# Three small moves in a two-layer kernel: expert sums scaled on ScalarE, filler matmuls on TensorE, the last group of the last stage split over two engines

## The chip, the cores and the metric

One core of one Trainium2 chip runs the whole kernel as a single program. The time is device microseconds (us) of that core. The engines are named as in the profile: PE is TensorE (PEld its weight loads), DVE is VectorE, ACT is ScalarE, POOL is GpSimd, SP is SyncE (it only issues DMAs here). L1305 is line 1305 of the kernel before.

## The reference, cut to what matters

4096 tokens of width 128 (2 sequences of 2048) go through four blocks, each as `x = x + layernorm(block(layernorm(x)))`:

```python
x = x + _layernorm(_L0_attn_ref(_layernorm(x)))   # state-space scan, 16 states, over 2048 steps
x = x + _layernorm(_L0_ffn_ref(_layernorm(x)))    # 8 experts, each takes its 512 best tokens
x = x + _layernorm(_L1_attn_ref(_layernorm(x)))   # linear attention, 8 heads of 16, Taylor features
x = x + _layernorm(_L1_ffn_ref(_layernorm(x)))    # 8 experts, each token goes to its best 2
```

The layernorm is `(x - mean) / sqrt(var + 1e-5)` over the 128 features. Everything is fp32.

## The kernel before, in words

The tokens lie on the chip in `X`, 8 groups of 512 tokens (4 tiles of 128 each, `J` = 4, `W` = 512). Each engine has its own instruction stream, written out by hand in the order in which that engine is to do it; streams meet only at semaphores (`wait_ge`). Where a step serves several groups at once, `groups` and `each_group` call it with offsets: `at(0)` is the group of this step, `at(1)` and `at(2)` the next ones, `at(-1)` and `at(-2)` those before. An engine does a step's instructions strictly in the order written, so one that waits holds up all behind it.

The layer-1 attention (scan): PE turns and projects the tokens, DVE makes the scan (L1045 to L1060) and signals `a_hc`. PE then makes outputs in 4 chunks `c` of two sequences `b`: `skips(c)` (the `D * x` term, 8 products of 128 columns, L1595) and `outputs(c)` (8 products with 32 rows, L1602) into PSUM. `skips(0)` and `skips(1)` stand ahead of the wait for `a_hc`. DVE takes the statistics of each (chunk, sequence) (`stats`, L989 to L997), POOL the `-0.5` power, DVE adds the normalised output to `X` (L1080) and takes statistics of the sum; ACT writes the normalised rows (L801), PE turns these (`scores`, L1611) and, when ACT has copied them (L808), multiplies by the router's weights (L1616). ACT copies the scores out (L812). The rows of the last (chunk, sequence) are made by DVE (L1092). The last scores go by a DMA (L816) to the search for the experts' thresholds.

The key pass of the layer-2 attention has 8 steps, one a group, over four engines. Before it the experts' sums are loaded into `acc` (two buffers). Per step, with m = at(0), g = at(1), h = at(2):
- DVE (L1293 to L1334): for g the shift (L1311) and `X += acc * rstd`, four `scalar_tensor_tensor` of 128x128 (L1315); products of m's tile 0 (L1305, L1307); statistics of `X` of g; statistics of `acc` of h; the shift of g (`shift`, L1277); products of m's tiles 1 to 3.
- POOL (L697): power for g (`d_xrstd`), power for h (`d_frstd`, the one by which `acc` is scaled), a product for the logits.
- ACT (L865): eviction of m's four tiles from PSUM (L876, L878) and of the queries (L885), then for g `normalise` (four `activation`, L858), then when PE has turned these, the copy `xnT` (L896).
- PE (L1723): the projections of m (L1730, L1754), the accumulations (L1740), the turning of g (L1763).

The choice of experts of layer 2: after the last group's `mix`, DVE clears `scan[:, 0:1]` (L1438) and casts `choice_b` (L1439), then scans the counts (L1441). When the lists are done (`r_lists`), POOL starts the gathers of the last block (L733), behind four waits, `r_lists` the first (L722 to L725).

The last stage (`finish`): for each of 8 groups the two choices' rows are added (DVE L1547 for the first 4, PE L1918 into a PSUM bank for the last 4: `ysum` products with the identity, 512 columns), DVE takes the statistics, POOL makes the factor (`g_rstd`) and the shift (`g_nmr`), ACT scales four tiles in place (L978) and signals `g_out`, DVE adds to `X` (L1556), and SP stores. DVE does the add of group n two steps after its statistics.

## Time and profile before

| | us |
|---|---|
| median of 3 runs | 719.86 (718.79 to 723.21) |
| the profiled execution | 715.17 |
| its span, first to last instruction | 713.3 |
| PE busy | 518.2 (73%) |
| DVE busy | 426.9 (60%) |
| ACT busy | 332.8 (47%) |
| POOL busy | 313.0 (44%) |
| mean granted TensorE clock | 0.847 |

The profiled execution is 1.87 us longer than its span and 4.69 us under the median of the runs. Times inside the span are counted from its start. A row of the timeline merges neighbouring instructions of one line: start, length, engine, line, what is written and read, count, and in brackets how long the engine sat idle before it and what ended that. An fp32 product on PE stands as two MATMUL records. PEclk is the granted TensorE clock, 1.00 for 2.4 GHz and 0.50 for 1.2 GHz.

### The profile page before, as it was taken

How to read it: one execution, taken by the hardware profiler on the slowest of the kernel's cores; microseconds unless marked ns; L12 is line 12 of the kernel's file. 1: busy time of each engine (PE TensorE's matmuls, PEld its weight loads, DVE VectorE, ACT ScalarE, POOL GpSimd, SP SyncE). 2: the span in 40 equal slices, each digit the busy share in tenths (PEclk: the TensorE clock that was granted, in tenths of full speed). 3: DMA queues.
4: the chain of work that ended last, by engine and by line, in shares of the span. 5: the costliest groups of instructions: out<-in, count | busy, mean ns of one | idle time of the engine just before them, and what ended most of it. 6: DMA issues, size and time to landing. Idle time of an engine off the chain costs nothing.

```text
span 713.3 us, 13599 instructions
## 1 busy us (share of the span) xinstructions
PE 518.2 (73%) x3894; PEld 382.3 (54%) x3896; DVE 426.9 (60%) x1784; ACT 332.8 (47%) x690; POOL 313.0 (44%) x329
## 2 busy tenths in 40 slices
PE   1769610378777508877899997149999999999925
PEld 1457100245544303433334444149999999999921
DVE  4789668835322238898426878883545545455447
ACT  3815510044323115454357663165666666666616
POOL 3514300067878723243001112016777667767535
PEclk9966755569978758899999998559999999999976
DMA  7401272012323350100000100021111111111155
GB/s 189 130 0 56 69 291 123 6 38 41 45 43 43 34 173 28 31 15 1 2 0 16 31 27 20 15 24 42 50 48 49 46 47 48 48 44 49 38 202 167
DMA packets 47736, 42.23 MB, mean 59 GB/s; under 512 B 15346, under 2 KB 41835, under 8 KB 47179
## 3 DMA queue, kind: packets, MB, share of 16 engines
q1 hardware_dynamic: 35770, 25.48, 11.4%
q0 software_dynamic: 10816, 15.82, 10.6%
q10 hardware_dynamic: 1104, 0.39, 0.2%
q8 instruction: 21, 0.34, 0.2%
q14 instruction: 25, 0.20, 0.1%
HBM read 26.23 MB, written 15.30 MB: 58 GB/s over the span
## 4 chain that ended last, share of the span: by engine, by line
PE 45%; DVE 27%; issue 11%; POOL 6%; ACT 5%; DMA 4%; ACTq 1%; DVEq 0%; POOLq 0%; SPq 0%
PE bank L1886 18%; PE bank L1907 9%; DVE st L1259 3%; POOL sum_dram L673 3%; PE bank L1695 2%; PE bank L1740 2%; PE bank L1730 2%; DVE mv L1264 2%; POOL arena L661 2%; DVE st L989 2%; ACT arena L913 1%; POOL rstd L687 1%; PE bank L1796 1%; DVE hit L1103 1%; PE bank L1896 1%
## 5 line engine op out<-in xcount | busy, mean ns | idle before, releaser
L1886 PE MATMUL bank<-arena 128*128 128x128 f32 x1136 | 140.1, 277 | 0.4 <-ACT arena L964 0.4
L1886 PEld LDWEIGHTS bank<-arena 128*128 128x128 f32 x1136 | 133.9, 194 | 0.7 <-ACT arena L964 0.7
L687 POOL TENSOR_TENSOR rstd<-ve,mhalf 128x4 f32<-128x4 f32 x40 | 48.7, 1217 | 167.7 <-DVE ve L1267 121.7
L1519 DVE TENSOR_TENSOR arena<-arena,bank 128x512 f32<-128x512 f32 x71 | 48.8, 688 | 81.4 <-PE bank L1886 81.4
L741 POOL DMA_INDIRECT y_dram<-arena,sidx x71 | 69.9, 985 | 44.4 <-DVE arena L1524 41.1
L950 ACT ACTIVATE arena<-wgu 128x1024 f32 x71 | 75.0, 1057 | 26.5 <-PE bank L1886 26.2
L733 POOL DMA_INDIRECT arena<-x3row_dram,gidx x71 | 68.8, 969 | 36.5 <-issue 20.7
L1907 PE MATMUL bank<-w,arena 128*128 x568 | 75.1, 275 | 0.0
L1907 PEld LDWEIGHTS bank<-w,arena 128*128 128x128 f32 x568 | 69.1, 192 | 0.2 <-issue 0.2
L956 ACT ACTIVATE arena<-bank 128x512 f32<-128x512 f32 x71 | 42.4, 597 | 42.7 <-PE bank L1886 42.7
L673 POOL DMA_INDIRECT sum_dram<-arena,idx x32 | 50.7, 1585 | 15.2 <-issue 7.6
L661 POOL DMA_INDIRECT arena<-x1row_dram,idx x32 | 31.3, 977 | 59.0 <-DMA x1row_dram<-wtok 49.0
L1241 DVE TENSOR_TENSOR arena<-arena,bank 128x256 f32<-128x256 f32 x32 | 13.5, 421 | 62.9 <-ACT arena L845 52.5
L913 ACT ACTIVATE arena<-bank 128x512 f32<-128x512 f32 x64 | 33.0, 603 | 22.4 <-PE bank L1796 22.4
L1305 DVE TENSOR_TENSOR arena<-arena 128x1024 f32<-128x1024 f32 x32 | 39.1, 1223 | 7.2 <-ACT arena L876 6.9
L1695 PE MATMUL bank<-w,arena 128*128 128x512 f32 x64 | 39.4, 702 | 0.0
L1740 PE MATMUL bank<-arena 128*17 128x153 f32 x512 | 25.5, 324 | 14.2 <-DVE arena L1307 14.1
L1524 DVE TENSOR_SCALAR arena<-bank,wrow 128x128 f32<-128x128 f32 x71 | 24.9, 351 | 11.4 <-PE bank L1907 7.0
L1740 PEld LDWEIGHTS bank<-arena 128*17 128x17 f32 x512 | 12.7, 103 | 32.4 <-issue 18.0
L1632 PE MATMUL bank<-cntb,blk_b 128*128 128x3 bf16 (+1 forms) x17 | 3.2, 186 | 35.7 <-DVE rank L1103 30.0
L1730 PE MATMUL bank<-wqkv,xnf 128*128 128x328 f32 x64 | 26.3, 519 | 1.0 <-ACT xnf L896 0.7
L1690 PE MATMUL bank<-ident,arena 128*128 128x128 f32 x32 | 11.1, 347 | 21.0 <-DMA arena<-x1row_dram,idx 21.0
(326 smaller groups left out, 1049.0 us busy)
## 6 DMA issues: line engine op xcount, KB each, us to landing
wgu<-in_wgu SPq DMA_DIRECT2D x1, 4096.0 KB, 12.2
wgu<-y_dram SPq DMA_DIRECT2D x8, 512.0 KB, 6.7
X<-in_x SPq DMA_DIRECT2D x8, 256.0 KB, 5.6
sum_dram<-zero POOLq DMA_DIRECT2D x8, 256.0 KB, 4.2
x1row_dram<-row SPq DMA_DIRECT2D x8, 256.0 KB, 2.4
w<-in_w SPq DMA_DIRECT2D x1, 2048.0 KB, 17.4
acc<-sum_dram SPq DMA_DIRECT2D x8, 256.0 KB, 2.9
w<-in_wd SPq DMA_DIRECT2D x1, 2048.0 KB, 10.2
```

What stands on the lines that cost most here:

```text
L661: nc.gpsimd.indirect_dma_start(xg[:, n % XG], None, x1row_dram, bass.IndirectOffsetOnAxis(ap=idx[:, e, k:k + 1].bitcast(U32), axis=0)).the ...
L673: nc.gpsimd.indirect_dma_start(sum_dram, bass.IndirectOffsetOnAxis(ap=idx[:, e, k:k + 1].bitcast(U32), axis=0), yw[:, n % 8], None, comput ...
L687: nc.gpsimd.tensor_tensor(out, ve[:, u], mhalf[:, 0:J], ALU.pow).then_inc(done, 1)
L733: nc.gpsimd.indirect_dma_start(xr[:, n.ring], None, x3row_dram, bass.IndirectOffsetOnAxis(ap=gidx1[:, n.n:n.n + 1].bitcast(U32), axis=0)). ...
L741: nc.gpsimd.indirect_dma_start(y_dram, bass.IndirectOffsetOnAxis(ap=sidx1[:, o.n:o.n + 1].bitcast(U32), axis=0), yr[:, o.ring], None).then ...
L950: nc.scalar.activation(wnow[:, k.pair], wgu[:, ds(e, 1)].rearrange("p o n -> p (o n)"), ACT.Copy).then_inc(f_w, 1)
L956: nc.scalar.activation(sgl[:, m.pair], bank[1 + m.pair][:], ACT.Silu).then_inc(f_silu, 1)
L1519: nc.vector.tensor_tensor(gl[:, m.pair], sgl[:, m.pair], bank[3 + m.pair][:], ALU.mult).then_inc(f_gated, 1)
L1695: nc.tensor.matmul(bank[2 + m.pair][:], xgT[:, m.pair], w13[:, ds(m.lap, 1)].rearrange("p o n -> p (o n)"), start=True, stop=True).then_in ...
L1740: last = nc.tensor.matmul(bank[3 + a.b][32 * q:32 * q + DH + 1, g_ * NF:(g_ + 1) * NF], vx[:, j, h, 0:DH + 1], kx[:, j, h, 0:NF], start=Fa ...
L1886: last = nc.tensor.matmul(bank[first + m.pair][:, h * P:(h + 1) * P], wnow[:, m.pair, at_:at_ + P], xrT[:, m.ring], start=True, stop=True)
L1907: last = nc.tensor.matmul(bank[5 + o.pair][:, 0:D], gl[:, o.pair, h * P:(h + 1) * P], wd[:, ds(e, 1), h].rearrange("p o n -> p (o n)"), st ...
```

## The change

- Key pass: ACT scales `acc` of h by `rstd` in place (four `activation` Copy with a per-partition scale), placed between `normalise` of g and the `xnT` copy of g, and signals `d_scaledsum`; DVE waits for it and does one `tensor_tensor` add of 128x512 in place of the four of L1315.
- TensorE: `keep_warm(n)` issues n products of the identity with `xnTA[:, 0, 0]` (128x512, fp32) into bank 6, which nobody reads. Nine stand behind `skips(1)` and ahead of the wait for `a_hc`, five ahead of `scores(3)`.
- Last stage, last group: DVE scales tiles 2 and 3 from the bank straight onto `X`, signals `g_scaled`, and adds their shift; ACT waits for `g_scaled` and scales tiles 0 and 1 only; DVE then adds 256 columns in place of 512.
- The clearing of `scan` and the cast of `choice_b` move into the last step of the query pass, ahead of DVE's wait for `q_yrstd`.
- POOL's wait for `r_lists` becomes the last of the waits ahead of the first gather.
- `g_scaled` and `d_scaledsum` are semaphores used earlier (`g_sum`, `a_abs`), counted on.

```diff
+        g_scaled, SCALED_BY_DVE = g_sum, GR - BY_DVE
+        d_scaledsum, SCALED = a_abs, CH
...
-            pool.wait_ge(r_lists, LEAD + 2)
             for u in range(2):
                 pool.wait_ge(q_rowst[u], LEAD + 16 * CH)
             pool.wait_ge(f_wst, LEAD + 16)
+            pool.wait_ge(r_lists, LEAD + 2)
...
             def key_pass(at):
-                g, m = at(1), at(0)
+                h, g, m = at(2), at(1), at(0)
...
                     normalise(lambda j: xn[:, g.b, j], tokens(g), g.b).then_inc(d_xn, 1)
+                if h:
+                    act.wait_ge(d_frstd, LEAD + h.n + 1)
+                    for j in range(J):
+                        last = nc.scalar.activation(acc[:, h.b, j], acc[:, h.b, j], ACT.Copy, scale=rstd[:, h.b, j:j + 1])
+                    last.then_inc(d_scaledsum, 1)
+                if g:
                     act.wait_ge(d_xtps, LEAD + g.n + 1)
                     if not early(g, 2):
                         act.wait_ge(d_qkv, LEAD + J * (g.n - 1))
                     nc.scalar.activation(xnT[:, g.b], bank[0][:], ACT.Copy).then_inc(d_xt, 1)
-            groups(act, key_pass, 1, 0, 2)
+            groups(act, key_pass, 2, 0, 2)
...
                 act.wait_ge(g_nmr, LEAD + g.n + 1)
-                for j in range(J):
+                if g.n == GR - 1:
+                    act.wait_ge(g_scaled, LEAD + SCALED_BY_DVE + 1)
+                for j in range(J if g.n < GR - 1 else 2):
...
-                    for j in range(J):
-                        xc = xl[:, ds(g.place, 1), j].rearrange("p o d -> p (o d)")
-                        last = nc.vector.scalar_tensor_tensor(xc, acc[:, g.b, j], rstd[:, g.b, j:j + 1], xc, ALU.mult, ALU.add)
-                    last.then_inc(d_x2, 1)
+                    dve.wait_ge(d_scaledsum, LEAD + SCALED + g.n + 1)
+                    xc = X[:].rearrange("p b c w -> p (b c) w")[:, ds(g.place, 1)].rearrange("p o w -> p (o w)")
+                    nc.vector.tensor_tensor(xc, xc, acc[:, g.b].rearrange("p j d -> p (j d)"), ALU.add).then_inc(d_x2, 1)
...
                 if m:
+                    if m.n == GR - 1:
+                        nc.vector.memset(scan[:, 0:1], 0.0)
+                        nc.vector.tensor_copy(choice_b[:], choice128[:])
                     dve.wait_ge(q_yrstd, LEAD + m.n + 1)
...
-            nc.vector.memset(scan[:, 0:1], 0.0)
-            nc.vector.tensor_copy(choice_b[:], choice128[:])
             dve.wait_ge(r_counts, LEAD + 1)
...
+                if l and l.n == GR - 1:
+                    dve.wait_ge(g_rstd, LEAD + l.n + 1)
+                    for j in range(2, J):
+                        last = nc.vector.scalar_tensor_tensor(xl[:, l.place, j], bank[l.n][:, j * P:(j + 1) * P],
+                                                              rstd[:, l.b, j:j + 1], xl[:, l.place, j], ALU.mult, ALU.add)
+                    last.then_inc(g_scaled, 1)
+                    dve.wait_ge(g_scaled, LEAD + SCALED_BY_DVE + 1)
+                    dve.wait_ge(g_nmr, LEAD + l.n + 1)
+                    for j in range(2, J):
+                        nc.vector.tensor_scalar(xl[:, l.place, j], xl[:, l.place, j], nmr[:, l.b, j:j + 1], None, ALU.add)
                 if l:
                     dve.wait_ge(g_out, LEAD + l.n + 1)
-                    x = xl[:, l.place].rearrange("p j d -> p (j d)")
-                    nc.vector.tensor_tensor(x, x, (ysum[:, l.n, 0] if l.n < BY_DVE else bank[l.n])[:, 0:W], ALU.add).then_inc(g_x, 1)
+                    w = W if l.n < GR - 1 else 2 * P
+                    x = xl[:, l.place].rearrange("p j d -> p (j d)")[:, 0:w]
+                    nc.vector.tensor_tensor(x, x, (ysum[:, l.n, 0] if l.n < BY_DVE else bank[l.n])[:, 0:w], ALU.add).then_inc(g_x, 1)
...
+            def keep_warm(n):
+                for _ in range(n):
+                    nc.tensor.matmul(bank[6][:], ident[:], xnTA[:, 0, 0], start=True, stop=True)
             skips(0)
             skips(1)
+            keep_warm(9)
             pe.wait_ge(a_hc, LEAD + 1)
...
                     outputs(c + 2)
+                if c == CH - 1:
+                    pe.wait_ge(a_x1t, LEAD + 2 * c)
+                    keep_warm(5)
                 scores(c)
```

## Rows read from the trace of the kernel before

**Rows 1.** The page, its part 4: shares of the chain by engine

```profile
PE 45%; DVE 27%; issue 11%; POOL 6%; ACT 5%; DMA 4%; ACTq 1%; DVEq 0%; POOLq 0%; SPq 0%
```

**Rows 2.** Stretches: length; busy PE, PEld, DVE, ACT, POOL; PEclk, DMA share, GB/s

```profile
50.10:76.40 26.30, 22.06 (x101) 16.23 (x100) 24.98 (x178) 12.44 (x28) 13.00 (x13) 0.69 0.16 44
...
258.00:344.00 86.00, 62.70 (x620) 31.60 (x624) 73.56 (x285) 38.61 (x112) 30.59 (x40) 0.85 0.12 38
```

**Rows 3.** Timeline of PE around the wait for the scan

```profile
37.78 3.59 PE L1595 MATMUL bank<-diagD,arena 128*128 128x128 f32 x16 [2.46 <-DVE arena L1032]
46.28 6.50 PE L1602 MATMUL bank<-wout,arena 32*128 32x128 f32 x32 [4.91 <-DVE arena L1060]
...
67.75 2.05 PE L1602 MATMUL bank<-wout,arena 32*128 32x128 f32 x16
```

**Rows 4.** Stretches of PE alone: length; busy (records); PEclk, DMA share, GB/s

```profile
41.00:44.40 3.40, 0.37 (x3) 0.99 0.00 0
44.60:64.90 20.30, 18.07 (x75) 0.50 0.09 26
```

**Rows 5.** The chain in order of time: two 512-column products at full clock

```profile
30.10 1.73 PE bank L1581 x4
```

**Rows 6.** Timeline of DVE: statistics of the first two outputs

```profile
48.40 0.29 DVE L989 BATCH_NORM_STATS2 st<-bank 128x6 f32<-128x128 f32 x1 [2.17 <-issue]
...
50.10 0.29 DVE L989 BATCH_NORM_STATS2 st<-bank 128x6 f32<-128x128 f32 x1 [0.20 <-issue]
```

**Rows 7.** All waits of DVE from 50.1 to 76.4: total, times, longest

```profile
DVE st L989 <- issue: 0.2, 1, 0.2
```

**Rows 8.** Timeline of PE at the end of the stage (scores of chunks 2 and 3)

```profile
79.39 3.18 PE L1616 MATMUL bank<-x1T,wg 128*8 128x512 f32 x4
84.78 0.66 PE L1611 MATMUL bank<-ident,row 128*128 128x128 f32 x4 [2.21 <-ACT row L801]
...
87.08 2.75 PE L1616 MATMUL bank<-x1T,wg 128*8 128x512 f32 x4
```

**Rows 9.** Timeline of ACT in the key pass: one step, and a later half-clock step

```profile
283.37 1.65 ACT L858 ACTIVATE xnf<-X,nmr,rstd 128x128 f32<-128x128 f32 x4 [0.18 <-DVE nmr L1277]
286.00 0.60 ACT L896 ACTIVATE xnf<-bank 128x512 f32<-128x512 f32 x1 [0.98 <-PE bank L1763]
287.77 0.33 ACT L876 ACTIVATE arena<-bank 128x192 f32<-128x192 f32 x1 [1.17 <-PE bank L1730]
...
296.72 0.60 ACT L896 ACTIVATE xnf<-bank 128x512 f32<-128x512 f32 x1 [2.01 <-PE bank L1763]
```

**Rows 10.** Timeline of POOL: the power of the next group's sums, same step

```profile
283.42 1.92 POOL L687 TENSOR_TENSOR rstd<-ve,mhalf 128x4 f32<-128x4 f32 x1 [0.22 <-DVE ve L1267]
```

**Rows 11.** Timeline of DVE: the first group's add, and one step's

```profile
259.16 1.13 DVE L1315 SCALAR_TENSOR_TENSOR X<-acc,rstd,X 128x128 f32<-128x128 f32 x4
...
287.21 1.13 DVE L1315 SCALAR_TENSOR_TENSOR X<-acc,rstd,X 128x128 f32 x4
288.26 1.21 DVE L1305 TENSOR_TENSOR arena<-arena 128x1024 f32<-128x1024 f32 x1
```

**Rows 12.** Groups of ACT by shape: busy us, mean ns, idle before

```profile
L830 ACT ACTIVATE arena<-arena,pcol 128x512 bf16<-128x512 bf16 x8 | 5.8, 722 | 42.2 <-DVE arena L1197 42.2
...
L789 ACT ACTIVATE arena<-arena 128x512 f32<-128x512 f32 x1 | 0.6, 631 | 0.0
```

**Rows 13.** Timeline of the last group of the last stage

```profile
708.35 1.48 ACT L978 ACTIVATE bank<-bank,nmr,rstd 128x128 f32<-128x128 f32 x4 [0.54 <-POOL nmr L754]
709.86 0.69 DVE L1556 TENSOR_TENSOR X<-X,bank 128x512 f32<-128x512 f32 x1 [1.33 <-ACT bank L978]
```

**Rows 14.** Timeline: cast ahead of the scan of counts, and the first gather

```profile
455.59 0.19 DVE L1439 CAST arena<-choice 128x64 bf16<-128x64 f32 x1
...
455.69 0.68 DVE L1441 TENSOR_TENSOR_SCAN arena<-onesW,bank 128x256 f32<-128x256 f32 x1
...
478.02 1.07 POOL L733 DMA_INDIRECT arena<-x3row_dram,gidx  x1 [13.71 <-DVE gidx L1501]
```

## The prediction

> **What bounds the kernel now.** I read the page first, then the chain in order of time, then the timeline engine by engine at the places touched. The page's chain says that no single engine sets the time: PE 45%, DVE 27%, POOL 6%, ACT 5% [rows 1]. So each edit has to be read in its own stage. The long expert stage, where PE is the bound, is not touched. The edits lie in four others:
> - The scan stage of layer 1. From 50.1 to 76.4 DVE is busy 24.98 of 26.30 us, PE 22.06 [rows 2], and DVE's waits there add up to 0.2 us, all of it one wait [rows 7]. DVE sets the pace; PE only matters at the start and at the end.
> - The key pass of layer 2. DVE is busy 73.56 of 86.00 us and ACT only 38.61 [rows 2]. That looks like work to be moved from DVE to ACT. But the loop through a step is DVE's shift, ACT's normalise, PE's turning, ACT's copy, PE's projection, ACT's eviction, DVE's products, so ACT's place in it counts, not its share.
> - The choice of experts and the last stage: short chains.
>
> **Nine fillers ahead of the outputs.** PE ends `skips(1)` at 37.78 + 3.59 = 41.37 and sits idle 4.91 us until the scan is done at 46.28 [rows 3]. A filler is an fp32 product with 512 columns. At full clock two of these took 1.73 us [rows 5], so 0.865 each; nine take 7.8 us. The clock is granted at 0.99 from 41.0 to 44.4 and at 0.50 from 44.6, after PE has stood idle [rows 4]; with fillers in that gap I take it as staying full. The fillers then end at 41.37 + 7.8 = 49.15, 2.9 us after the scan. The first sequence's outputs are 8 records; at full clock 16 took 2.05 us [rows 3], so 1.03. DVE starts at 49.15 + 1.03 + 0.05 = 50.2, against 48.40. The second statistics started at 50.10 after 0.20 of idle time [rows 6], which goes: so +1.8 - 0.2 = +1.6 us on DVE, which has no slack behind it until 76.4 to win it back. Faster products afterwards win nothing, since DVE doesn't wait for them [rows 7]. Bounds: if `skips(1)` ran at full clock (2.05 for 16 records) PE would be free 1.5 us earlier and the loss is 0.1; if the clock falls at 44.5 all the same, it is 7.5 (below). I take 1.6.
>
> **Five fillers ahead of the last scores.** PE ends the scores of chunk 2 at 79.39 + 3.18 = 82.57 and gets the next rows at 84.78 [rows 8]. Five fillers at full clock take 4.3 us and end at 86.9, 2.1 us after the rows. The two turnings follow at 0.6 each, the second copy of ACT at 0.6 runs beside the first product, and two score products at full clock take 1.73: 86.9 + 0.6 + 0.6 (copy of the first) + 1.73 = 89.8. Before, the last product pair was 2.75 us, partly at half clock, and ended at 87.08 + 2.75 = 89.83 [rows 8]. So 0.0. Bounds: -0.7 if the pair before would have been wholly at half clock (2 x 1.73 = 3.46), and +2 if the fillers begin at half clock. I take 0, because the warm products pay back just what the fillers take.
>
> **The key pass.** The price of a scale on ACT is not in the trace with this form. A Copy with one per-partition operand took 722 ns for 512 columns, one with immediates 631 [rows 12], so an operand costs 91 ns. Four 128-column instructions with two operands take 1.65 us [rows 9]: 0.39 from start to start. One operand less gives 0.30, and four give 1.3 us; bounds 0.8 (no price for the operand) and 1.65. On DVE four instructions took 1.13 us and the next starts 1.05 after the first [rows 11]; one add of 512 columns is 0.69 [rows 13], some 0.61 from start to start. DVE wins 0.44 us a step.
>
> Now where ACT does it: after `normalise` of g, before the copy `xnT` of g. In the step shown ACT is done with normalise at 285.0; POOL's power for h ends at 283.42 + 1.92 = 285.34 [rows 10], so ACT waits for it, behind it the copy waits, and behind that PE's projections. The scales run 285.4 to 286.6, the copy starts at 286.6 instead of 286.00 [rows 9]: +0.6. The eviction that DVE needs ended at 287.77 + 0.33 = 288.10, DVE started its products at 288.26 [rows 9, 11]: 0.16 of slack, so +0.44 on the products of tile 0. From these to the next shift nothing shrinks, so the loop grows by 0.44. What DVE saved (0.44) it now waits away ahead of these products. Seven steps have a scale. Four run at full clock (this one; the other three, worked the same way, +0.31 to +0.40): together 1.5. In the others the turning itself is late because PE is at half clock: there the copy starts 3.5 us after normalise began or later (296.72, after 2.01 us of idle time) [rows 9], which covers the scales: 0. A rule of the Trainium skill speaks here against the change: "ScalarE: Activation LUTs", rules for kernel authors, puts multiply and add on VectorE, not ScalarE. By that rule the four scales stay where they were and the sum would be 2.4 us lower; the trace agrees insofar as ACT's four cost 1.3 us where DVE saves 0.44.
>
> The first group has no step ahead of it to hide in. There the chain is POOL's power, DVE's add at 259.16 (1.13) [rows 11], statistics. Now it is power, four scales (1.3), add (0.69): +0.9. Key pass: 1.5 + 0.9 = +2.4. Bounds: -2.2 (scales quite hidden, seven steps at -0.44, first group +0.9), and +5.8 (seven steps at +0.7).
>
> **The last stage.** DVE is free at 709.86 - 1.33 = 708.53 [rows 13]. It scales two tiles (0.28 each from rows 11) until 709.15. ACT waits for that instead of starting at 708.35: two tiles, half of 1.48 plus a start, from 709.2 to 710.0 [rows 13]. DVE's two shifts lie beside it. The add of 256 columns is some 0.4: 710.4 to 710.45, against 710.55. So -0.1, bounds -0.3 to +0.3. Cutting ACT's work in half is nearly eaten by ACT's later start.
>
> **The two reorders.** The cast stood 0.10 us ahead of the scan of counts [rows 14]; ahead of `q_yrstd` it lies in DVE's wait for POOL's power: -0.1 (0 if that wait is short). The first gather starts 0.28 us after the list's last instruction, at 478.02 [rows 14]; three passed waits less behind the last signal: -0.05, bounds -0.2 and 0.
>
> **Sum.** 1.6 + 0 + 2.4 - 0.1 - 0.1 - 0.05 = +3.75, say +3.7. The profiled execution took 715.17, so 718.9 for one like it. The median of the runs shown is 4.69 above it; I add the sum to the median: 719.86 + 3.7 = 723.6.
>
> **Rivals.**
> - DVE stays the bound of the key pass and the scales are hidden. For it: DVE's 86% against ACT's 45%. Against: the products of tile 0 follow the eviction by 0.16 only, and the copy is behind the scales in order. Key pass -2.2 instead of +2.4: 719.0.
> - The fillers carry the full clock to the end of the scan stage. For it: this is what they are placed for, and PE at full clock from 76 would cut the two score pairs from 3.18 and 2.75 to 1.73 each, -2.4: 721.2. Against: PE idles between chunks whatever stands at 41. The Trainium skill ("TensorE: Matmul & The Clock Gate", why this matters for your kernels) says that continuous work keeps the clock up; the trace doesn't bear that out for this work: from 44.6 to 64.9 PE was busy 18.07 of 20.30 us at 0.50 [rows 4].
> - The other side, slower: the clock falls at 44.5 in spite of the fillers. Then 3.1 us of fillers (3.6 of them) run at full clock, 5.4 at 1.73 take 9.3: they end at 53.8. The outputs at half clock add 2.1: DVE starts at 55.9 instead of 48.40, +7.5 instead of +1.6: 729.5. It decides above 1% from the point where more than four of the nine run at half clock. Against: the clock rose by 41.0 on the products of `skips(1)`, and wider ones should hold it.
>
> **Chances.** Forecast 0.60, hidden scales 0.15, full clock to the end 0.11, clock falls 0.10, something else 0.04. About 1% (7.2 us) is what a measurement can tell from no change. The gains even of both good rivals together (716.6) stay within it, so faster by over 1% gets 0.03; slower has the third rival and the upper ends of the key pass and the last scores: 0.13; the rest, 0.84, is within 1%. The range goes from 717.5 (first rival, with the good ends of the small terms) to 729.5 (third rival).
>
> **What would show it.** In the scan stage: the nine fillers end near 49, PE's first L1602 products at full clock, and DVE's wait ahead of the first statistics 3.9 us instead of 2.17. In the key pass: ACT's wait for POOL between normalise and scales, the copy some 3.4 us after normalise starts, DVE idle about 0.8 us ahead of the products of each tile 0, and the full-clock steps 0.4 us longer than before. In the last stage: DVE ends within 0.3 us of before, counted from the first statistics. I am wrong if the fillers end before 47, if DVE doesn't wait in the key pass, or if those steps are shorter than before.

## The result, and the profile after

| | before | after |
|---|---|---|
| median | 718.73 us (715.70 to 723.21, 20 runs) | 723.52 us (717.42 to 729.34, 20 runs) |
| ratio of the two | | 1.0059, 95% interval 1.0041 to 1.0076 |
| profiled execution | 715.17 us, span 713.3 | 725.88 us, span 724.0 |
| mean granted clock | 0.847 | 0.852 |

The change costs 0.59% (0.41 to 0.76), some 4.2 us; the medians differ by 4.79. The forecast was +3.7 us and 723.6. One of the 20 executions after, the one of 729.34 us, ran in a slower state of the chip and is left out of the ratio. The two profiled executions lie 10.7 us apart. That is more than the medians differ by: single executions scatter over 7.5 us before and 8.5 after (without the slow one). Of the 10.7 us, 2.9 lie in the scan stage and 3.8 in the key pass; the other 4 are spread over stages that the change hardly touches. So below a stage is compared over several profiles, and a part of the change by its ratio.

The page after, its part 4, answers to [rows 1]:

```profile
PE 46%; DVE 25%; issue 10%; POOL 6%; DMA 6%; ACT 6%; ACTq 1%; DVEq 0%; POOLq 0%; SPq 0%
```

Still no engine sets the time. What DVE gave up in the chain (27% to 25%) went to PE, ACT and DMA.

**The scan stage.** PE of the kernel after, timeline, answers to [rows 3]:

```profile
41.49 8.07 PE L1640 MATMUL bank<-arena,ident 128*128 128x512 f32 x18
49.48 1.38 PE L1623 MATMUL bank<-wout,arena 32*128 32x128 f32 x10
```

DVE of the kernel after, answers to [rows 6]:

```profile
45.92 0.69 DVE L1070 TENSOR_TENSOR arena<-arena 128x512 f32<-128x512 f32 x1
50.69 0.29 DVE L999 BATCH_NORM_STATS2 st<-bank 128x6 f32<-128x128 f32 x1 [4.07 <-issue]
```

The scan is done at 46.61; the nine fillers (18 records) keep PE until 49.5. DVE idles 4.07 us instead of 2.17.

Stretches of the kernel after, for [rows 4] (length; busy PE, PEld, DVE, ACT, POOL; PEclk; DMA share, GB/s):

```profile
42.00:50.00 8.00, 8.00 (x22) 3.56 (x21) 4.41 (x7) 0.00 (x0) 0.00 (x0) 1.00 0.00 0
50.00:54.00 4.00, 2.98 (x30) 2.79 (x28) 3.16 (x25) 0.00 (x0) 1.34 (x2) 1.00 0.00 0
54.00:58.00 4.00, 2.05 (x11) 1.75 (x12) 3.84 (x24) 0.00 (x0) 1.71 (x2) 0.69 0.00 2
58.00:66.00 8.00, 8.00 (x33) 6.47 (x33) 7.61 (x56) 4.38 (x10) 4.03 (x4) 0.50 0.22 66
```

The granted clock is 1.00 until about 55.5 (a mean of 0.69 from 54 to 58 is 1.5 us at 1.00 and 2.5 at 0.50). Behind the fillers PE was busy 2.98 of the 4 us from 50 to 54. Then it is 1.2 GHz, also for a stretch in which PE is busy all 8.00 us. From 50 to 76 the full clock could buy nothing: DVE sets the pace there, and after the 4.07 us it has no other wait up to 76.8.

The tail, PE of the kernel after, for [rows 8]:

```profile
84.90 5.19 PE L1640 MATMUL bank<-arena,ident 128*128 128x512 f32 x10
89.93 1.04 PE L1632 MATMUL bank<-ident,row 128*128 128x128 f32 x8
91.21 1.88 PE L1637 MATMUL bank<-x1T,wg 128*8 128x512 f32 x4 [0.25 <-ACT x1T L810]
```

The five fillers take 5.19 us where 4.3 was worked out, so a part of them ran at half clock. They end at 90.1, after the rows are there, and the turnings and the last products behind them run at full clock (1.04 and 1.88).

**The key pass.** ACT in one step of the kernel after, for [rows 9]:

```profile
288.37 1.65 ACT L860 ACTIVATE xnf<-X,nmr,rstd 128x128 f32<-128x128 f32 x4 [0.17 <-DVE nmr L1287]
290.37 1.28 ACT L898 ACTIVATE acc<-acc,rstd 128x128 f32<-128x128 f32 x4 [0.35 <-POOL rstd L689]
291.56 0.57 ACT L904 ACTIVATE xnf<-bank 128x512 f32<-128x512 f32 x1
```

DVE in the same step, for [rows 11], the first group's add ahead of it:

```profile
264.69 0.69 DVE L1325 TENSOR_TENSOR X<-X,acc 128x512 f32<-128x512 f32 x1 [1.14 <-ACT acc L898]
...
292.21 0.68 DVE L1325 TENSOR_TENSOR X<-X,acc 128x512 f32 x1
294.43 1.23 DVE L1315 TENSOR_TENSOR arena<-arena 128x1024 f32<-128x1024 f32 x1 [1.54 <-ACT arena L878]
```

ACT waits for POOL, then scales, and its copy starts 291.56 - 288.37 = 3.19 us after `normalise` began; before it was 286.00 - 283.37 = 2.63 [rows 9]. DVE ends its add early and then idles 1.54 us for the eviction.

**The last group**, timeline of the kernel after, for [rows 13]:

```profile
716.05 0.29 DVE L1269 BATCH_NORM_STATS2 st<-bank 128x6 f32<-128x128 f32 x1
...
719.40 0.60 DVE L1566 SCALAR_TENSOR_TENSOR X<-bank,rstd,X 128x128 f32<-128x128 f32 x2
720.04 0.48 DVE L1572 TENSOR_SCALAR X<-X,nmr 128x128 f32<-128x128 f32 x2
720.10 0.78 ACT L988 ACTIVATE bank<-bank,nmr,rstd 128x128 f32<-128x128 f32 x2 [1.34 <-DVE X L1566]
720.91 0.42 DVE L1577 TENSOR_TENSOR X<-X,bank 128x256 f32<-128x256 f32 x1 [0.39 <-ACT bank L988]
```

The same place in the kernel before, to count from:

```profile
705.12 0.29 DVE L1259 BATCH_NORM_STATS2 st<-bank 128x6 f32<-128x128 f32 x1
```

Counted from the last group's first statistics the last add starts 0.12 later than before (720.91 - 716.05 = 4.86 us against 709.86 - 705.12 = 4.74), but it has 256 columns fewer and ends 0.15 sooner (5.28 against 5.43). From these statistics to the end of the span it is 7.98 to 7.99 us in the four profiles with the split and 8.14 to 8.16 in the ten without: -0.15.

### The profile page after: what moved, and what is told of

Its sections match the earlier page's. It is cut to its first block, busy times and chain, and to the rows that moved or that the text cites. A ratio compares the mean times of both kernels' runs of the same rounds, so it can differ in the third digit from the quotient of the medians.

```text
span 724.0 us, 13673 instructions
## 1 busy us (share of the span) xinstructions
PE 530.0 (73%) x3922; PEld 384.2 (53%) x3924; DVE 424.3 (59%) x1764; ACT 341.8 (47%) x720; POOL 313.7 (43%) x329
## 4 chain that ended last, share of the span: by engine, by line
PE 46%; DVE 25%; issue 10%; POOL 6%; DMA 6%; ACT 6%; ACTq 1%; DVEq 0%; POOLq 0%; SPq 0%
PE bank L1914 18%; PE bank L1935 9%; DVE st L1269 3%; POOL sum_dram L675 3%; PE bank L1758 3%; PE bank L1768 2%; PE bank L1723 2%; POOL rstd L689 2%; POOL arena L663 2%; DVE mv L1274 2%; DVE st L999 1%; ACT arena L921 1%; PE bank L1824 1%; PE bank L1924 1%; DVE hit L1113 1%
## 5 line engine op out<-in xcount | busy, mean ns | idle before, releaser
L663 POOL DMA_INDIRECT arena<-x1row_dram,idx x32 | 31.4, 981 | 59.9 <-DMA x1row_dram<-wtok 49.8
L1251 DVE TENSOR_TENSOR arena<-arena,bank 128x256 f32<-128x256 f32 x32 | 13.5, 422 | 63.9 <-ACT arena L847 55.5
L1315 DVE TENSOR_TENSOR arena<-arena 128x1024 f32<-128x1024 f32 x32 | 39.2, 1224 | 11.2 <-ACT arena L878 9.3
L1534 DVE TENSOR_SCALAR arena<-bank,wrow 128x128 f32<-128x128 f32 x71 | 24.9, 351 | 11.3 <-PE bank L1935 6.6
```

The costliest lines, as they stand in the source:

```text
L663: nc.gpsimd.indirect_dma_start(xg[:, n % XG], None, x1row_dram, bass.IndirectOffsetOnAxis(ap=idx[:, e, k:k + 1].bitcast(U32), axis=0)).the ...
```

## The experiments

Each ratio is to the kernel before, timed beside it on the same chip (medians 717.93, 716.54 and 718.40 in the three sets that ran together).

| kernel | ratio | 95% interval |
|---|---|---|
| fill9_only | 1.0055 | 1.0020 to 1.0089 |
| fill5_only | 1.0009 | 0.9979 to 1.0039 |
| fill5_gap | 1.0011 | 0.9988 to 1.0034 |
| key_only | 1.0054 | 1.0031 to 1.0076 |
| key_late | 1.0053 | 1.0033 to 1.0073 |
| key_late_first | 1.0065 | 1.0048 to 1.0082 |
| key_free | 0.9999 | 0.9977 to 1.0021 |
| key_dummy | 1.0026 | 1.0003 to 1.0050 |
| rest_only | 1.0007 | 0.9981 to 1.0034 |
| order_only | 1.0015 | 0.9992 to 1.0038 |
| no_fill | 1.0047 | 1.0027 to 1.0067 |
| full | 1.0057 | 1.0026 to 1.0089 |

### The fillers

**fill9_only**: of the change only

```diff
             skips(1)
+            keep_warm(9)
             pe.wait_ge(a_hc, LEAD + 1)
```

> The kernel before plus only the nine filler products ahead of the wait for the scan. Theory (the fillers are longer than the gap): they end 7.8 us after skips(1) at full clock, DVE's wait ahead of the first statistics is 3.9 to 4.1 us instead of 2.17, and from the scan's end (end of L1060) to the first count of the threshold search the time grows by 1.6 to 2.0 us; whole kernel +0.1% to +0.4%. Rival 1 (the clock kept high pays back): the same stretch is not longer than before (47.4 us from the scan's end to the first count). Rival 2 (the clock falls in spite of the fillers): DVE's wait is 6 us or more.

Measured 722.02 us, +0.55% (0.20 to 0.89), more than the 0.1% to 0.4% expected, with an interval that takes these in. From the scan's end to the first count of the search: 50.19 us, before 47.36. That is +2.8 where 1.6 to 2.0 was expected. The wait of DVE is the 4.08 us of the change. What I had not counted is the tail. PE in fill9_only, timeline:

```profile
87.25 2.37 PE L1611 MATMUL bank<-ident,row 128*128 128x128 f32 x8 [2.21 <-ACT row L801]
89.55 3.58 PE L1616 MATMUL bank<-x1T,wg 128*8 128x512 f32 x4
```

The rows arrive at 87.25 where they came at 84.78 [rows 8]; counted from the scan's end (46.68 and 46.22) that is 40.57 against 38.56, so 2.0 us later. The last products take 3.58 (wholly at 1.2 GHz) instead of 2.75: 0.8 more. Together the 2.8 us. The second term is no price of the fillers: in four of the nine profiles without any filler in this stage (rest_only, order_only, key_dummy, key_late_first) the last products also took 3.58. In these nine the stretch is 46.9 to 48.1 us, mean 47.5, with the same code. The three profiles with the nine fillers have 50.19 (fill9_only), 50.24 (after) and 48.97 (full), mean 49.8: the fillers cost 2.3 us here, between 1.4 and 2.7.

**fill5_only**:

```diff
+                if c == CH - 1:
+                    pe.wait_ge(a_x1t, LEAD + 2 * c)
+                    keep_warm(5)
                 scores(c)
```

> The kernel before plus only the five filler products ahead of scores(3). Theory: they hold back the last turnings by about 2 us and the products after them run at full clock; from the rows' arrival to the first count the stretch is between 0.7 us shorter and 2 us longer than before, most likely +0.0 to +0.9 (the traces of the whole change showed +0.86, with part of the fillers at half clock). Rival (they pay, as the full clock takes more off the last four product records than the fillers delay them): shorter by over 0.3 us.

Measured 717.38 us, +0.09% (-0.21 to +0.39); the stretch is 47.29 against 47.36 us. PE in fill5_only, timeline:

```profile
81.62 4.56 PE L1619 MATMUL bank<-arena,ident 128*128 128x512 f32 x10
86.01 1.04 PE L1611 MATMUL bank<-ident,row 128*128 128x128 f32 x8
87.30 1.88 PE L1616 MATMUL bank<-x1T,wg 128*8 128x512 f32 x4 [0.25 <-ACT x1T L808]
```

The fillers take as much as the warm products give back. In the change the same is seen against fill9_only: the last products end at 93.09 with the five fillers and at 93.13 without. Against the nine profiles without fillers (46.9 to 48.1) no gain or loss below some 0.6 us could be told.

**fill5_gap**: five fillers in the gap, so that they end before the scan does, and none later

```diff
             skips(1)
+            keep_warm(5)
             pe.wait_ge(a_hc, LEAD + 1)
```

> Five filler products instead of nine ahead of the wait for the scan, none later. Five take 4.3 us at full clock and PE's gap is 4.9 us. Theory (the nine cost because they are longer than the gap; the clock they hold is worth something): PE starts the outputs as soon as the scan is done, at full clock, DVE's wait ahead of the first statistics is 1.1 to 1.3 us (2.17 before, 4.08 with nine), and the stretch from the scan's end to the first count is 0.5 to 1.4 us shorter than the 47.4 before. Rival (the fillers are of no use at all): the wait is 2.1 us or more and the stretch is 47.2 or longer.

PE and then DVE in fill5_gap, timeline:

```profile
41.03 5.18 PE L1619 MATMUL bank<-arena,ident 128*128 128x512 f32 x10
46.74 3.17 PE L1602 MATMUL bank<-wout,arena 32*128 32x128 f32 x27 [0.53 <-DVE arena L1060]
```

```profile
47.94 0.29 DVE L989 BATCH_NORM_STATS2 st<-bank 128x6 f32<-128x128 f32 x1 [1.25 <-issue]
```

DVE starts 0.9 us sooner than before, as the idea behind fillers promises. But the stretch to the first count is 47.36, that of before and not the 0.5 to 1.4 less that was expected, and the kernel is at +0.11% (-0.12 to +0.34). Of the 0.9 us, 0.8 are still there when the last rows arrive (37.7 us after the scan's end against 38.56). Then the last products ran at half clock (3.58 against 2.75) and took them back. The four profiles without fillers whose last products took 3.58 as well have 48.0 to 48.1: beside these fill5_gap is 0.6 to 0.7 shorter. So the expected gain is there in the trace, a single one, and the ratio can't show it.

### The key pass

**key_only**: the scales on ACT between `normalise` and the copy, DVE's one add.

```diff
+                if h:
+                    act.wait_ge(d_frstd, LEAD + h.n + 1)
+                    for j in range(J):
+                        last = nc.scalar.activation(acc[:, h.b, j], acc[:, h.b, j], ACT.Copy, scale=rstd[:, h.b, j:j + 1])
+                    last.then_inc(d_scaledsum, 1)
```

> The kernel before with only the key pass changed (ACT scales the experts' sums between normalise and the xnT copy). Theory (the scales stand in the loop ACT, PE, ACT, DVE): the key pass, from the first statistics of the sums to DVE's copy of the accumulated sums (88.0 us before), grows by 2.4 to 4 us, and DVE waits 0.8 us or more ahead of tile 0's products in every step at full clock; whole kernel +0.3% to +0.6%. Rival (DVE's work is the bound, the growth in the whole change came from another place): the key pass is shorter by up to 2.2 us.

Measured 721.24 us, +0.54%. Waits of DVE in the key pass of key_only (us in total, times, longest):

```profile
DVE arena L1313 <- ACT arena L878: 9.2, 7, 1.8
DVE X L1323 <- ACT acc L898: 2.8, 2, 1.7
```

The kernel before:

```profile
DVE arena L1305 <- ACT arena L876: 6.9, 5, 3.1
```

Now DVE waits for the eviction in seven steps, not in five, and for the scales in the first two. The key pass takes 91.77 us, +3.8 over before (2.4 to 4 expected) and +2.5 over the mean of six unchanged passes (below).

**key_late**: the same scales behind the copy. The expectation holds my theory at that point: it is ACT's order that costs, so with the copy early again the loss should go.

```diff
                     nc.scalar.activation(xnT[:, g.b], bank[0][:], ACT.Copy).then_inc(d_xt, 1)
+                if h:
+                    act.wait_ge(d_frstd, LEAD + h.n + 1)
...
+                    last.then_inc(d_scaledsum, 1)
```

> The key pass as in the change, but ACT scales the sums after the copy xnT, not ahead of it. Theory (it was the place in ACT's order that cost): the copy starts as early as before, the scales (1.3 us) fit between it and the next eviction (1.8 us later before), and only the first group's +0.8 us is left: key pass 88.0 to 89.5 us against 91.8 in the change, kernel at most +0.15% over before. Rival (ACT's added work as such costs, wherever it stands): key pass 91 us or more, kernel +0.4% or more.

The theory fell: 721.39 us, +0.53%, no better. ACT, then DVE, in one step of key_late:

```profile
285.99 0.60 ACT L898 ACTIVATE xnf<-bank 128x512 f32<-128x512 f32 x1 [0.98 <-PE bank L1769]
286.49 1.26 ACT L902 ACTIVATE acc<-acc,rstd 128x128 f32<-128x128 f32 x4
```

```profile
287.90 0.69 DVE L1322 TENSOR_TENSOR X<-X,acc 128x512 f32 x1 [0.63 <-ACT acc L902]
289.36 1.22 DVE L1312 TENSOR_TENSOR arena<-arena 128x1024 f32<-128x1024 f32 x1 [0.77 <-ACT arena L878]
```

The copy starts 2.62 us after `normalise` (283.37), as early as before. But the scales now end at 287.75 and DVE, which wants the sums at 287.27, waits for them. Waits of DVE in key_late:

```profile
DVE X L1322 <- ACT acc L902: 11.7, 8, 3.5
DVE arena L1312 <- ACT arena L878: 2.1, 4, 0.8
```

The wait has changed its name and is no smaller: 11.7 + 2.1 = 13.8 us, against 9.2 + 2.8 = 12.0 in key_only. The pass takes 92.17 us where at most 89.5 was expected. POOL's factor comes about 2.2 us after DVE's shift (`nmr`), DVE wants the sums 4.0 us after it, and within these 1.8 us ACT has the scales (1.3) and the copy (0.6) to do: one of the two is late, and whichever it is, DVE waits.

**key_late_first**: key_late, with the first group's sums scaled by DVE as before. Against key_late:

```diff
-                if h:
+                if h and not first(h):
...
+                    if first(g):
+                        for j in range(J):
...
+                    else:
+                        dve.wait_ge(d_scaledsum, LEAD + SCALED + g.n)
...
```

> As key_late, and the first group is scaled and added by DVE as in the kernel before. Theory: the 0.8 us of the first group go too: from the first statistics of the sums to the first statistics of X 3.9 us as before instead of 4.7, key pass 0.8 us shorter than in key_late, kernel the same as before or up to 0.2% faster. Rival: as for key_late.

Measured +0.65% (0.48 to 0.82), with a key pass of 91.50, where a kernel no slower than before was expected: the rival's numbers. The first group itself came out as worked out: from the first statistics of the sums to the first of `X` it is 3.91 us here and in before, 4.70 in the five profiles in which ACT scales the first group too. That is 0.8, too small for the ratios to show.

**key_free**: nobody scales the sums (the scaling by `rstd` is left out), DVE does the one add.

```diff
-                        last = nc.vector.scalar_tensor_tensor(xc, acc[:, g.b, j], rstd[:, g.b, j:j + 1], xc, ALU.mult, ALU.add)
...
+                    nc.vector.tensor_tensor(xc, xc, acc[:, g.b].rearrange("p j d -> p (j d)"), ALU.add).then_inc(d_x2, 1)
```

> Key pass as in key_only, but nobody scales the expert sums: ScalarE has no scales, VectorE still adds 512 columns at once (the scaling of the sums is left out). It shows what the shorter add is worth when nothing is put on ScalarE. Theory A (the loop through a step sets the pace, VectorE only fills a wait of some tenths): the 0.44 us saved in a step are waited away ahead of the products of tile 0 but for the 0.16 of slack; key pass 87 to 88.5 against 88.02, ratio 0.998 to 1.001. Rival (VectorE is the bound of the key pass): 8 x 0.44 = 3.5 us less, key pass 84.5, ratio 0.995.

Measured 717.86 us, ratio 0.9999 (0.9977 to 1.0021). The rival's 0.995 is out of the interval. By the interval what DVE saves is worth at most 0.23%, or 1.7 us, even when it costs nothing elsewhere, and not the 3.5 us of an engine that sets the pace: VectorE is not the bound of this pass, with 86% busy. The trace has a gain in the first group (3.46 us against 3.91) and in the second step (9.02 against 9.38 to 9.95 in six unchanged passes), and none in the rest; the pass took 89.41, above the expected 87 to 88.5 and beside a mean of 89.3. DVE waits more instead. Waits of DVE in key_free:

```profile
DVE arena L1308 <- ACT arena L878: 10.1, 6, 3.6
```

**key_dummy**: DVE as before, ACT scales a constant into a buffer that nobody reads.

```diff
+                if h:
+                    act.wait_ge(d_frstd, LEAD + h.n + 1)
+                    act.wait_ge(d_scaledsum, LEAD + SCALED + h.n)
+                    for j in range(J):
+                        last = nc.scalar.activation(yn[:, 1, j], ident[:], ACT.Copy, scale=ident[:, 0:1])
+                    last.then_inc(d_scaledsum, 1)
```

> The key pass as before on VectorE (four scale-and-adds), with four scales of 128 columns of a constant into an unused buffer on ScalarE at the place where the change has its own, behind the same wait for POOL; nobody waits for them. Theory A (what costs is that ScalarE stands behind POOL's power and its copy comes late, so that the granted clock of TensorE falls in most steps too): key pass 91 to 92, ratio 1.004 to 1.006, as key_only. Rival (what costs is VectorE's wait for ScalarE's scaled sums): key pass 88 to 89, ratio 0.999 to 1.001.

Measured 720.74 us, +0.26% (0.03 to 0.50), key pass 90.87. The rival (what costs is DVE's wait for the sums) allowed at most +0.1% and 89; theory A asked for +0.4% to +0.6% and 91 to 92. The result is between them, and its interval takes in both. The key pass can't decide either: one of the six unchanged passes (fill5_gap) took 91.47. One part of the cost has a name all the same. ACT and DVE in a step of key_dummy:

```profile
285.34 1.28 ACT L899 ACTIVATE yn<-ident 128x128 f32<-128x128 f32 x4 [0.35 <-POOL rstd L689]
286.52 0.57 ACT L905 ACTIVATE xnf<-bank 128x512 f32<-128x512 f32 x1
```

```profile
283.15 0.15 DVE L1286 SCALAR_TENSOR_TENSOR nmr<-mv,rstd 128x4 f32<-128x4 f32 x1
...
289.38 1.23 DVE L1314 TENSOR_TENSOR arena<-arena 128x1024 f32<-128x1024 f32 x1 [1.08 <-ACT arena L878]
```

In this step DVE's products of tile 0 start 6.23 us after its shift; in the change 294.43 - 288.18 = 6.25; before 288.26 - 283.18 = 5.08. And DVE idles 1.08 us ahead of them with its long add, 1.54 with the short one: the 0.46 us between the two is the whole saving of the change, waited away. Only the first group, where the change also waits 1.14 us for the scales, is missing in key_dummy.

**Steps of the key pass.** DVE's shift (`nmr`) stands once in each step. From its first to its seventh in the pass, that is over six steps, the profiles give:

| kernels | scales on ACT | six steps, us | short ones of the third to sixth | seventh step, us |
|---|---|---|---|---|
| before, rest_only, order_only | no | 59.78, 60.72, 60.65 | 3, 2, 2 | 10.16, 9.20, 9.69 |
| fill9_only, fill5_only, fill5_gap | no | 61.90, 61.33, 61.67 | 0, 1, 0 | 9.71, 9.96, 10.32 |
| key_free (no scaling) | no | 61.77 | 0 | 9.96 |
| key_dummy, key_only, no_fill | yes | 62.68, 62.82, 63.58 | 0, 0, 0 | 10.12, 10.09, 9.36 |
| key_late, key_late_first | yes | 63.79, 63.91 | 0, 0 | 9.52, 9.52 |
| full, after | yes | 63.21, 63.60 | 0, 0 | 10.00, 9.37 |

The first of the six steps is 9.9 us in all fourteen. The mean of the six unchanged key passes (the first two lines) is 61.0, of the seven with scales 63.4: +2.4 us. From the third to the sixth step, short ones of 9.44 to 9.72 us are found without scales, beside others of 10.2 to 11.3; but fill9_only, fill5_gap and key_free have none either. With scales all four take 10.5 to 11.3. In the granted clock these short steps stand at 1.00 and the long ones at 0.70 to 0.85. Where a step keeps its 1.00, scales ahead of the copy cost little: in the second step 9.86 us with them against 9.67 without (means of five and six profiles), in the seventh 9.37 (after, no_fill) against 9.20 (rest_only). The whole pass, from the first statistics of the sums to the copy of PE's results, is 88.0 to 91.5 us unchanged (mean of six 89.3) and 91.8 to 92.2 with the key pass of the change (key_only, no_fill, full, after; mean 91.9): +2.6. PE in the third step of key_only shows what makes a step long:

```profile
286.37 0.66 PE L1770 MATMUL bank<-ident,xnf 128*128 128x128 f32 x4
287.12 1.09 PE L1747 MATMUL bank<-arena 128*17 128x153 f32 x16
288.33 1.46 PE L1737 MATMUL bank<-wqkv,xnf 128*128 128x328 f32 x2
```

And the same place in the kernel before:

```profile
285.31 0.66 PE L1763 MATMUL bank<-ident,xnf 128*128 128x128 f32 x4
286.06 0.71 PE L1740 MATMUL bank<-arena 128*17 128x153 f32 x16
286.74 0.81 PE L1730 MATMUL bank<-wqkv,xnf 128*128 128x328 f32 x2
```

A projection that DVE's next products hang on takes 1.46 us in place of 0.81. The copy costs 0.55 us and the slower projection 0.6; together 5.08 becomes 6.25. From 278 to 338, PE in the kernel before and then in key_only (length; busy PE; PEclk; DMA share, GB/s):

```profile
278.00:338.00 60.00, 46.73 (x486) 0.91 0.07 19
```

```profile
278.00:338.00 60.00, 47.23 (x444) 0.86 0.06 19
```

But the clock falls right after the turning, before the late copy is felt: in both kernels PE was idle 2.01 us ahead of the accumulation before that turning, and one kept 2.4 GHz and the other lost it. key_free, with no scales at all, also lost it in this step. So the fall is not the scales' own work in this step. What the seven profiles show is that a pass with scales had no short step from the third to the sixth, while the seventh was short again in four of them (9.36 to 9.52). Three of seven passes without scales had none either, so it isn't shown that the scales are what takes the clock away; why it is lost there is open. A kernel that keeps PE busy in that gap was not tried.

### The rest

**rest_only**: the two reorders and the split of the last group, neither fillers nor key pass; of its diff

```diff
+                    if m.n == GR - 1:
+                        nc.vector.memset(scan[:, 0:1], 0.0)
+                        nc.vector.tensor_copy(choice_b[:], choice128[:])
...
-                for j in range(J):
+                for j in range(J if g.n < GR - 1 else 2):
```

> The kernel before with the two reorders and the split of the last group, no fillers and the key pass as before. Theory: -0.1 us for the cast, -0.1 us for the last group, nothing for the order of POOL's waits: no change that can be measured (within 0.2%). Rival (the order of POOL's waits costs): the first gather starts 1.0 us after the last list instruction (end of gidx) instead of 0.27 us as before, so +0.5 to +0.8 us in the profile.

**order_only**: of these only POOL's waits.

```diff
-            pool.wait_ge(r_lists, LEAD + 2)
             for u in range(2):
                 pool.wait_ge(q_rowst[u], LEAD + 16 * CH)
             pool.wait_ge(f_wst, LEAD + 16)
+            pool.wait_ge(r_lists, LEAD + 2)
```

> The kernel before with only the order of POOL's four waits changed (r_lists last). Theory, from the four traces with the old order and the two with the new: the DMA of the choices' weights lands within a few tenths of the lists, and after it lands the new order costs more ahead of the gather than the old one. The first gather then starts 0.9 to 1.1 us after the end of the gidx instruction where the DMA lands last (0.54 to 0.57 with the old order), 0.3 where the lists come last; whole kernel within 0.2%. Rival (the order is free, the 0.4 us lie in when the DMA lands): from the landing of that DMA to the gather it takes as long as in fill5_only and fill9_only.

Measured +0.07% (-0.19 to +0.34) and +0.15% (-0.08 to +0.38): both can't be told from nothing. The traces can say more. From the last group's first statistics to the end of the span rest_only takes 7.99 us and before 8.14. The first gather gained nothing, and in order_only it lost. Its chain, in order of time:

```profile
479.11 0.21 DVE gidx L1501
...
479.39 0.81 issue
480.19 2.78 DMA arena<-x3row_dram,gidx
```

The gather starts 0.88 us after the end of the lists' last instruction (479.32), though the DMA of the tokens' weights (32 KB, L595 here) had landed at 478.50, 0.81 ahead of that end. With the old order and the lists at least as far behind the landing it was 0.28 (before) and 0.29 (fill5_gap, key_late_first, key_only). In the kernel after the DMA comes last:

```profile
479.59 6.89 DMA x3row_dram<-wts
...
486.61 0.81 issue
487.41 2.66 DMA arena<-x3row_dram,gidx
```

It lands at 486.48 (479.59 + 6.89), the lists end at 486.35, and the gather starts 0.93 after the landing. All fourteen profiles fit one pair of numbers for each order. With the old order the gather starts 0.28 us after the lists' end or 0.87 after the landing, whichever is later (nine profiles). With the new order it is 0.88 and 0.93 (five profiles). So the new order costs 0.6 us where the lists come last and 0.06 where the DMA does. The rival of rest_only expected 1.0 us after the lists' end and got 0.88: in the trace it is right, and the theory, nothing for the order, is not. In order_only both expectations fell: the theory asked for 0.3 where the lists come last, and the rival for 0.87 from landing to gather, where it took 1.69. Why POOL needs longer behind this wait is open. With the old order too the gather is late when the DMA is: up to 1.74 us after the lists' end in key_free, where the landing comes 0.87 after it.

### The whole and its parts

**no_fill**: the change without its fourteen fillers.

> The change without its fourteen fillers. If the costs of the parts add up as measured one by one (key pass 0.54%, the rest 0.07%): ratio 1.006, and the whole change should then be at 1.012. If the whole is what was measured (1.0059) and the nine fillers cost the 0.55% that they cost alone: ratio 1.000 to 1.001, with the key pass at 88 to 89. By my prediction: +2.1 us, 1.003.

**full**: the change once more, in the same set.

> The whole change once more, beside its own parts on the same chip. If the parts add up, 1.012; by the first comparison 1.0059 [1.0041, 1.0076]; by the prediction 3.7 us, 1.0052. Scan stage from the scan's end to the first count 50.2 against 47.4, key pass 91 to 92.

Measured 1.0047 (1.0027 to 1.0067) and 1.0057 (1.0026 to 1.0089). full repeats the first comparison (1.0059). In its trace the scan stage is 48.97 (50.2 expected) and the key pass 92.2. no_fill is what key pass and rest come to (0.54% + 0.07%), within its interval, and its key pass of 91.8 rules out the 88 to 89. But the parts one by one sum to 0.55 + 0.09 + 0.54 + 0.07 = 1.25%, and the whole is 0.59% and 0.57%. The fillers cost 0.55% alone and 0.10% on top of the rest, though the trace has 2.0 us more in the scan stage of full than in that of no_fill (48.97 against 46.95). Taken as independent, the four intervals give the sum +-0.57%, and the gap of 0.67% is hardly more; by the medians the parts come to 1.07% and the whole to 0.67% and 0.93%. So the gap may be chance. The stages in the traces (+2.3 in the scan stage, +2.6 in the key pass, up to +0.6 for POOL's order, -0.15 at the end) come to some 5 us or 0.7%, near the whole and not the 1.25%. No run settles whether the parts overlap.

## Why the prediction was right

The sign and the size came out: +4.2 us by the ratio (2.9 to 5.5), +3.7 forecast. That 723.6 and 723.52 differ by only 0.08 is luck: the forecast started from 719.86, the median of three runs, where 20 runs have 718.73, and by the medians the change is +4.79, so that a start 1.1 too high and a change 1.1 too low cancel. Step by step:

- **Nine fillers, +1.6.** The fillers ended at 49.5 (49.15 forecast), the outputs behind them ran at full clock, DVE waited 4.07 us: as worked out. The start of DVE moved by 1.9 us against the scan. The last rows came 2.0 later, so the 0.2 taken off for an idle time was not won back. The stage measured +2.8 alone, +2.9 in the change and +1.6 in full, against the single profile before; against the mean of nine profiles without fillers it is +2.7, +2.7 and +1.4. What differs is where the last products meet the clock. The rival in which the clock falls at 44.5 in spite of the fillers is out (1.00 until 54). So is the rival in which they carry the full clock on to 76: 0.50 from 58 to 66 with PE busy all the time. The rule of the Trainium skill named in the prediction ("TensorE: Matmul & The Clock Gate") would have it higher there, and the row stands against it once more.
- **Five fillers, 0.** Right within what one profile can show: 47.29 against 47.36 us. The mechanism too: they take what the warm products give back.
- **Key pass, +2.4.** The amount came out, its working did not. Of the signs, these came: ACT's wait for POOL (0.35), the scales at 1.28 us (1.3 forecast), the copy 3.19 us after `normalise` (3.2 by the working, 3.4 in the list of signs), the first group +0.8 (+0.9 forecast). key_free shows that the saved 0.44 us is not what the pass lacks, key_dummy beside it that it is waited away (0.46). Two signs missed: DVE's idle time ahead of the products is 1.54 us in place of 0.8, and a full-clock step did not become 0.4 us longer but went from 9.5 to 10.7. The step that failed is "four full-clock steps +1.5, half-clock steps 0", which left the clock where it was in before. In a step that keeps its full clock the scales cost some 0.2, not 0.44. The price is in the steps that lose it: 0.55 for the copy and about 0.6 for a projection at 1.2 GHz. Over six steps that is +2.3 in the four kernels with the change's own scales, where the prediction had 1.5. With the first group's +0.8, and -0.1 in the seventh step and -0.3 behind it (where one unchanged pass, fill5_gap, was slow), the whole pass is +2.6. That 2.4 came out so near is partly luck. Whether the scales cause the loss of the clock is not shown.
- **The price of a scale.** 1.3 us came out as 1.28, but the two rows it was read from differ in more than an operand: L830 is a Copy in bf16 and L789 an Exp in fp32.
- **What my own theory after the result got wrong.** Putting the scales behind the copy looked like a repair; key_late shows that the other neighbour, DVE's add, is as tight. In "ScalarE: Activation LUTs", rules for kernel authors, the Trainium skill puts such work on VectorE, and here it holds in each of the two places tried: 1.28 us on ACT to save DVE 0.46.
- **Last stage, -0.1.** It was -0.15: DVE's two scales took 0.60 and ACT's two 0.78, as worked out.
- **Reorders, -0.1 and -0.05.** The cast can't be seen. The wait order had the wrong sign: three passed waits fewer behind the last signal were to give 0.05, and the gather starts 0.6 us later behind the lists (order_only) or 0.06 behind the DMA of the weights. That DMA lands between 1.3 us before and 0.9 after the lists' end, and I had looked at the lists alone.

No version ran that beats the kernel before. The only part with a gain in the whole change's trace is the split of the last group, 0.15 us of 718, below what can be timed; alone it wasn't run.

## What to carry to other kernels

Before moving work from a busy engine to an idle one, look at what that engine's neighbours in order are waiting for. A share of 86% doesn't make an engine the bound: take the work away entirely first (key_free), and if nothing is gained, there is nothing for a move to win. Fillers that end after the data they wait for delay the path: here they ended 2.9 us late and DVE started 1.9 later, since the outputs behind them ran at full clock. The clock they hold is worth something only where PE sets the pace next. And before a stage of one profile is compared with that of another, look at how far profiles of unchanged code lie apart: 46.9 to 48.1 us in the scan stage here, 88.0 to 91.5 in the key pass.

## What was not expected of the hardware

- PE was busy 8.00 of 8.00 us from 58 to 66 with a granted clock of 0.50 in four profiles (after, full, fill9_only, fill5_gap). During the fillers of after, products of 512 columns, it was 1.00 (42 to 50, busy 8.00).
- Nearly the same PE work was followed by a fall of the clock in one profile and not in the other: from 283.2 to 286.2 PE is busy 1.44 us in the kernel before and 1.48 in key_dummy, and in the next microsecond the granted clock is 1.00 in the one and 0.50 in the other. Unchanged code in the key pass took 59.8 to 61.9 us for six steps. The 35 executions of the kernel before timed beside key_free had mean granted clocks from 0.835 to 0.855. The Trainium skill ("TensorE: Matmul & The Clock Gate", what's actually happening) says that the number of products before the first rise of the clock varies from run to run of one kernel; no run here shows that place, but these rows show the like for the falls in the middle of a kernel. A single profile of a stage like this can't price a change of 2 us.
- A DMA of only 32 KB, written as eight bytes a token, took 6.89 us from issue to landing in the kernel after, and 6.25 to 7.80 over the fourteen profiles; the first gather behind it took 2.66.
- With POOL's wait for the lists moved behind the three others, the first gather started 0.88 us after the lists' end in place of 0.28, though the last of the other waits had been met 0.8 us before that end (order_only).
